# One program text for all engines in a two-layer cross-attention kernel: value steps left whole, 63 pairs of row maxima joined

## The reference, cut to what matters

```python
q = (hidden_states @ Wq).reshape(B, Sq, HEADS, head_dim).transpose(0, 2, 1, 3)
k = (encoder_hidden_states @ Wk).reshape(B, Skv, HEADS, head_dim).transpose(0, 2, 1, 3)
v = (encoder_hidden_states @ Wv).reshape(B, Skv, HEADS, head_dim).transpose(0, 2, 1, 3)
scores = jnp.einsum('bhqd,bhkd->bhqk', q, k) / jnp.sqrt(jnp.asarray(head_dim, q.dtype))
probs = jax.nn.softmax(scores, axis=-1)
out = jnp.einsum('bhqk,bhkd->bhqd', probs, v)
out = out.transpose(0, 2, 1, 3).reshape(B, Sq, H) @ Wo + bo
return out + residual
```

## Time and profile before

| | |
|---|---|
| median of 3 runs | 323.26 us |
| span of the profiled execution | 320.5 us |
| median less span | 2.8 us |
| TensorE busy | 308.1 us (96%) |
| VectorE busy | 259.9 us (81%) |
| ScalarE busy | 228.9 us (71%) |
| GpSimd busy | 77.8 us (24%) |

### The profile page before, as it was taken

How to read it: one execution, slowest core, us unless ns; L and a number is a source line. 1 busy time by engine, 2 the same in 40 slices (tenths; PEclk the granted TensorE clock), 3 DMA queues, 4 the chain that set the end, 5 groups by cost and what they waited for, 6 DMA issues and landing times.

```text
span 320.5 us, 6083 instructions
## 1 busy us (share of the span) xinstructions
PE 308.1 (96%) x2086; PEld 166.4 (52%) x2086; DVE 259.9 (81%) x456; ACT 228.9 (71%) x468; POOL 77.8 (24%) x97
## 2 busy tenths in 40 slices
PE   7999999999999999999999999999999999999995
PEld 6678888876766634333344343334433453443335
DVE  1469899889986899998999899998999988893213
ACT  3556456543445797889878988888898877878982
POOL 6055157360434310010013100130441016101030
PEclk9999999999999999999999999999999999999999
DMA  7960007859946831471723817329065010110102
GB/s 228 322 200 0 2 2 199 246 142 179 225 127 204 183 80 54 95 107 52 125 60 76 126 42 124 75 68 125 27 124 92 37 50 30 57 33 26 38 30 83
DMA packets 20193, 32.79 MB, mean 102 GB/s; under 512 B 5539, under 2 KB 9667, under 8 KB 20163
## 3 DMA queue, kind: packets, MB, share of 16 engines
q1 hardware_dynamic: 19075, 31.27, 42.2%
q10 hardware_dynamic: 1088, 1.14, 1.2%
HBM read 20.63 MB, written 11.61 MB: 101 GB/s over the span
## 4 chain that ended last, share of the span: by engine, by line
PE 72%; ACT 9%; DVE 7%; issue 4%; DMA 4%; SPq 3%; POOL 1%; ACTq 0%; POOLq 0%; DVEq 0%
PE ps L1393 19%; PE ps L1370 13%; PE ps L1381 13%; PE ps L1221 10%; PE ps L1042 8%; ACT probs L701 4%; SPq L347 2%; ACT probs_last L701 2%; DVE mx L906 2%; PE ps L1108 2%; DMA QS<-mT 1%; DMA rec_rows<-recs 1%; PE ps L1168 1%; PE ps L1148 1%; DMA QS<-q_parts 1%
## 5 line engine op out<-in xcount | busy, mean ns | idle before, releaser
L906 DVE TENSOR_REDUCE mx<-ps 128x1 f32<-128x512 f32 x298 | 186.1, 683 | 16.3 <-PE ps L1370 14.6
L701 ACT ACTIVATE probs<-ps 128x512 f32<-128x512 f32 x216 | 113.5, 610 | 22.2 <-PE ps L1381 20.9
L1370 PE MATMUL ps<-KS,QS 48*128 48x512 f32 x256 | 77.9, 450 | 2.2 <-ACT probs L701 1.2
L1381 PE MATMUL ps<-QS,KS 50*128 50x512 f32 x256 | 72.1, 440 | 1.6 <-DMA QS<-mT 0.4
L1393 PE MATMUL ps<-probs,VS 128*32 128x512 f32 (+1 forms) x552 | 60.3, 511 | 0.3 <-ACT probs L701 0.3
L701 ACT ACTIVATE probs_last<-ps 128x512 f32<-128x512 f32 x104 | 54.8, 611 | 6.7 <-PE ps L1381 6.2
L1370 PEld LDWEIGHTS ps<-KS,QS 48*128 48x128 f32 x256 | 35.0, 184 | 36.8 <-DVE mx L906 16.2
L1381 PEld LDWEIGHTS ps<-QS,KS 50*128 50x128 f32 x256 | 33.9, 184 | 33.3 <-ACT probs L701 13.5
L1393 PE MATMUL ps<-probs_last,VS 128*32 128x512 f32 (+1 forms) x256 | 29.0, 524 | 0.0
L507 POOL CAST neg_p<-neg 128x16 fp32r<-128x16 f32 x10 | 2.1, 211 | 110.0 <-DVE neg L916 104.3
L683 ACT CAST parts<-ps 128x512 fp32r<-128x512 f32 (+1 forms) x18 | 10.5, 584 | 19.6 <-PE ps L1221 19.4
(11 more groups left out here) (186 smaller groups left out, 440.5 us busy)
## 6 DMA issues: line engine op xcount, KB each, us to landing
KS<-k_parts SPq DMA_DIRECT2D x48, 128.0 KB, 4.7
k_parts<-parts SPq DMA_DIRECT2D x8, 512.0 KB, 3.5
QS<-q_parts SPq DMA_DIRECT2D x48, 64.0 KB, 5.0
raw_rows<-o_raw SPq DMA_DIRECT2D x9, 256.0 KB, 2.0
q_parts<-parts SPq DMA_DIRECT2D x4, 512.0 KB, 3.9
cs<-in_ctx_dram SPq DMA_DIRECT2D x2, 768.0 KB, 9.3
KS_last<-k_parts SPq DMA_DIRECT2D x12, 128.0 KB, 4.6
xs<-in_x_dram SPq DMA_DIRECT2D x2, 640.0 KB, 6.3
```

Source lines behind the costliest of these rows:

```text
L701: act.activation(probs[t % 3][:, h, :], ps[:, bank_of["s", m], :], ACT.Exp, scale=float(D1) ** -0.5).then_inc(exp_done, 1)
L906: dve.tensor_reduce(mx[:, g % BUF, u:u + 1], ps[:, bank_of["m", n], :], AX.X, ALU.max).then_inc(max_done, 1)
L1370: pe.matmul(ps[:, bank, :], QS[g % BUF][rows, pair, qt * P:(qt + 1) * P], KS[g % BUF][rows, pair, half * 512:half * 512 + 512], start=True ...
L1381: pe.matmul(ps[:, bank, :], KS[g % BUF][rows, h // 2, kt * P:(kt + 1) * P], QS[g % BUF][rows, h // 2, :], start=True, stop=True).then_inc( ...
```

## The change

`EARLY`, `PLAN`, `BANKS`, `X_AT` and the rules of the other engines are gone. One text, `PROGRAM`, holds all units in order, and every engine walks it from front to back. Things that were tied to a step's number are now words in it: `o` (ScalarE or VectorE copies a group's output), `send`, `inv`, `pieces`, `chunk`, `stage`, `loadk`, `loadq`, `ones`, `bias0`. Where an order used to follow from the old list, waits are added (on `proj_mm`, `u_mm`, `x1_mm`, `q0_mm`). All 80 values steps are whole; 21 of them were cut before. `M` is a joined pair: 63 instead of 11. A group's value output may lie in any bank. s units may run ahead of the step by more or less than four. `sums` and `recs` have a place of their own in SBUF, and `sums_in` is two semaphores.

```diff
-    EARLY = [("warm", 0, 8), ("xT", 0, 0), ("xT", 0, 1), ("tok",), ("xT", 0, 2), ("w", 0), ("warm", 1, 8), ("kvp", 0), ("kvp", 1),
...
-    JOIN = [1, 5, 7, 39, 101, 173, 233, 263, 274, 295, 318]
-    PLAN = ["m1mmm203vmm", "201m3v", "1mm2m03vm", "m21m03v", "m21m0max3mmb", "m10mamm23bmm", "01mm2m3v", "3m210mmab", "10mmm32mmv",
...
+    PROGRAM = (
+        "bias0:0 warm:0:8 w:0 tok warm:1:8 xT:0:0 xT:0:1 xT:0:2 kvp:0 kvp:1 kvT:0 q0:0:0 q0:0:1 q0:0:2 n0:0 kvT:1 xT:1:0 xT:1:1",
...
+        "3m102mmvmmM301vmM012 loadq:3 3m3vm loadwo 2011mmv neg:1 send:0 MM032vMM02 o:0 1vmmm320 loadq:4 loadk:4 311mmv0mmm inv:0",
...
+    def parsed():
+
+        units, joined, n, m, v = [], set(), 0, 0, 0
+        for word in " ".join(PROGRAM).split():
+            if set(word) <= set("mMv0123ab"):
+                for c in word:
+                    if c in "mM":
+                        if c == "M":
+                            joined.add(n)
+                            units.append(("m", n))
+                            n += 1
+                        units.append(("m", n))
+                        n += 1
+                    elif c in "0123":
+                        units.append(("s", m, int(c)))
+                        m += 1
+                    else:
+                        units.append(("values", v, {"v": None, "a": 0, "b": 1}[c]))
+                        v += c != "a"
...
-            for u in EARLY:
-                leave(u)
-            for h in range(GH):
-                exp(h)
-            for t in range(STEPS):
...
+            for u in units:
+                leave(u)
...
-            def exp(m):
+            def exp(m, h):
...
                 if t >= 3:
                     act.wait_ge(pv_mm, t - 2)
+                elif m == 0:
+                    act.wait_ge(proj_mm, KV0_DONE)
+                elif m == 2 * GH:
+                    act.wait_ge(q0_mm, 6)
```

More of the change, by code:

```diff
@@ new lines, in two_layer_cross_attention @@
+    POOL_FROM = 8
+    def parsed():
[16 more added lines that the diff above has]
+                        v += c != "a"
+            else:
+                kind, *numbers = word.split(":")
+                units.append((kind, *(int(i) for i in numbers)))
+        return units, joined
@@ L101, in two_layer_cross_attention @@
+    units, JOIN = parsed()
     MAXIMA = list(itertools.accumulate(n not in JOIN for n in range(NM)))
-    NEG_STEP = [max([t for t in range(STEPS) if M_FROM[t] < (g + 1) * UNITS], default=-1) for g in range(NG)]
-    X_STEPS = {u: sorted(t for t in X_AT if X_AT[t] == u) for u in X_AT.values()}
+    head_of = {u[1]: u[2] for u in units if u[0] == "s"}
+    NO_BANK = ("loadk", "loadq", "w", "e0", "i0", "n0", "ones", "vones", "bias0", "o", "send", "inv", "pieces", "chunk", "stage",
+               "loadwo", "half", "finB")
@@ L110, in placed @@
         last_in[bank] = u
-    def heads(t):
-        return [int(c) for c in PLAN[t - 1] if c in "0123"] if t else [0, 1, 2, 3]
     def place_all():
-        early_banks = iter(EARLY_BANKS)
-        for u in EARLY:
[L119 to L135, removed]
-                    v += 1
-        for u, bank in zip((u for u in TAIL if u[0] != "finB" and u != ("finA", 7)), TAIL_BANKS):
-            placed(u, int(bank))
-        bank_of["finA", 7] = bank_of["res", 7]
+        banks = iter("".join(BANKS))
+        for u in units:
+            if u[0] == "values":
+                u = ("pv", u[1] // NKT) if u[1] % NKT == 0 and u[2] != 1 else ("values",)
+            if u[0] in NO_BANK or u[0] == "values":
+                continue
+            if u == ("finA", NT - 1):
+                bank_of[u] = bank_of["res", NT - 1]
+            elif u[0] == "m" and u[1] - 1 in JOIN:
+                placed(u, bank_of["m", u[1] - 1] + 1)
+            elif u[0] == "s":
+                placed(u[:2], int(next(banks)))
+            else:
+                placed(u, int(next(banks)))
     place_all()
@@ L151, in two_layer_cross_attention @@
     CHUNK = [(0, 1), (2, 3), (4,), (5, 6), (7, 8)]
-    O_STEP = [at // GH for at in O_AT] + [LATE_O]
+    KV0_DONE = max(proj_no[u] for u in proj_no if u[0] != "q" and u[1] == 0) + 1
+    KV1_DONE = max(proj_no[u] for u in proj_no if u[0] != "q" and u[1] == 1) + 1
+    Q0_DONE = max(proj_no[u] for u in proj_no if u[0] == "q" and u[1] == 0) + 1
     with ExitStack() as ctx:
@@ L579, in chunk_parts @@
                 pool.wait_ge(o_low, c + 1)
-            pool.wait_ge(vs_ready, 1)
-            stage_v(0)
-            for t in range(STEPS):
-                g, kt = t // NKT, t % NKT
-                for c, groups in enumerate(CHUNK):
-                    if t == O_STEP[groups[-1]] + 5:
-                        chunk_parts(c)
-                if kt == 5 and g + 1 < NG:
-                    stage_v(g + 1)
-                if t == WO1_AT:
-                    weight_low(WO1)
-                if t in [n for n in NEG_STEP if n >= 0]:
-                    neg_parts(NEG_STEP.index(t))
-                if t in X_AT and t == X_STEPS[X_AT[t]][-1]:
-                    u = X_AT[t]
-                    if u[0] in ("k", "q") and split_no[u] >= POOL_FROM:
-                        lower_part(u)
-                    elif u[0] == "fin" and u[1] < TB - 1:
-                        final(u[1])
+            for u in units:
+                if u[0] in ("k", "q") and split_no[u] >= POOL_FROM:
+                    lower_part(u)
+                elif u[0] == "m" and u[1] % UNITS == UNITS - 1:
+                    neg_parts(u[1] // UNITS)
+                elif u[0] == "w" and u[1] not in SPLIT_BY_DVE:
+                    weight_low(u[1])
+                elif u[0] == "n0":
+                    normalise0(u[1])
+                elif u[0] == "x1T":
+                    add_bias1(u[1])
+                elif u[0] == "ones":
+                    ones(u[1])
+                elif u[0] == "vones":
+                    value_ones()
+                elif u[0] == "bias0":
+                    add_bias0(u[1])
+                elif u[0] == "chunk":
+                    chunk_parts(u[1])
+                elif u[0] == "stage":
+                    stage_v(u[1])
+                elif u[0] == "fin" and u[1] < TB - 1:
+                    final(u[1])
         @block.scalar
@@ L741, in leave @@
                 if u[0] == "w":
+                    if u[1] == WO1:
+                        act.wait_ge(proj_mm, len(order))
                     weight_high(u[1])
+                elif u[0] == "s":
+                    exp(u[1], u[2])
+                elif u[0] == "o" and u[1] < NG - 2:
+                    copy_o(u[1])
+                elif u[0] == "half":
+                    copy_half(u[1])
+                elif u == ("finB", NT - 1):
+                    copy_last_sums(u[1])
                 elif u[0] == "ftB":
@@ L1019, in leave @@
                     add_last_chunk(u[1])
-            for u in EARLY:
-                leave(u)
-            for t in range(STEPS):
-                g, kt = t // NKT, t % NKT
-                if t == LATE_O:
-                    copy_late_o()
-                if t - 2 in O_STEP:
-                    invert_sums(O_STEP.index(t - 2))
-                for n in range(M_FROM[t], M_FROM[t + 1]):
-                    maximum(n)
-                if t in X_AT and t == X_STEPS[X_AT[t]][-1]:
-                    leave(X_AT[t])
-            for u in TAIL:
+            for u in units:
                 leave(u)
@@ L1321, in unit @@
                     scores(u[1])
+                elif u[0] == "values":
+                    values(u[1], u[2])
                 elif u[0] == "tok":
@@ L1388, in values @@
                 pe.wait_ge(exp_done, GH * t + GH)
-                if kt == 0:
+                if kt == 0 and half != 1:
                     pe.wait_ge(v_staged, g + 1)
@@ L1398, in _ @@
             pe.wait_ge(id_ready, 1)
-            for u in EARLY:
-                unit(u)
-            v = 0
-            for t in range(STEPS):
-                n, m = M_FROM[t], GH * (t + 1)
-                for c in PLAN[t]:
-                    if c == "m":
-                        max_scores(n)
-                        n += 1
-                    elif c in "0123":
-                        scores(m)
-                        m += 1
-                    elif c == "x":
-                        at = X_STEPS[X_AT[t]]
-                        unit(X_AT[t], *((at.index(t), len(at)) if len(at) > 1 else ()))
-                    else:
-                        values(v, {"v": None, "a": 0, "b": 1}[c])
-                        v += c != "a"
-            for u in TAIL:
+            for u in units:
                 unit(u)
```

147 lines of the change are left out of this document (56 added, 91 removed), and 52 rows, old and new, of tables (BANKS, EARLY, PLAN, PROGRAM).

## The result

The changed kernel takes 362.73 us (median of 4 runs, 357.89 to 364.74) against 323.02 us for the kernel before, run beside it (322.23 to 324.06). The ratio is 1.112, with an interval of 1.106 to 1.119: **slower by 11%**. The forecast was 320.6 us, and the range ended at 326.5. The profiled execution took 357.89 us, with a span of 356.2.

The account below looks back on a forecast made before the run. The prediction took VectorE's stream of maxima, 93% full with holes where TensorE comes late, to bound the main stage. Span 320.5 + 3.2 - 3.1 - 2.8 = 317.8, plus 2.8 to the median: 320.6 us; range 315.5 to 326.5.

Parts of the forecast that it names:

- The start: Before layer 0: query-weight work ahead of the token copies delays the first keys product, +3.2 us (bounds 0 and 5).
- Rival 3: TensorE's clock falls in a 2.6 us hole at the start, costing 1.9 us more: 322.5 us; chance 0.08.
- Joined pairs: Main stage, VectorE: each of 51 more joined maxima saves 0.06 us, 3.1 us off.
- All of it counts: Main stage: the full 3.1 us saved on VectorE by joins comes off the time, VectorE being 93% full.
- Rival 4: Main stage: joined pairs choke the banks and make TensorE late, slower, up to 326.5 us; chance 0.17.
- Whole steps: Main stage: 21 uncut values steps save TensorE 0.34 us each, 7.1 us; 2.8 counted, bounds 0 and 4.0.
- The main stage: First values step to last maxima: loses 5.9 us, 3.1 from joins plus 2.8 from TensorE's relief.
- the sign I gave for rival 4: Main stage: VectorE idle 13 us or more, most of it ahead of joined reductions.
- the 2.8 us: Main stage: TensorE's relief closes a fifth of VectorE's 13.2 us of idle time.
- The rest: Output copies, loads, GpSimd and SyncE queues, added waits and tail: nothing counted.
- The added waits, the loads: Added waits met long before; later groups' loads issued at least four values steps ahead of first m unit: nothing.
- The chance of slower: Whole kernel above 324.9 us: 0.20, from choked banks or a bad start with the clock falling or relief unused.

Follow-up runs that it names:

- section 4: section 3's kernel with neg:3, neg:6 earlier (321.16 us); that with maxima taken singly (322.51), 21 steps in halves (326.02), or the change's start (324.39).
- section 5's last kernel: Against section 4's first kernel: neg:3 takes another bank, inv:8 moved behind finC:7, stores of fin:2 and fin:3 later; 321.93 us, ratio 0.996.
- section 1: Kernel before the change with only GpSimd's first two chunks moved, one values step behind their group's output copy instead of five; 347.87 us against 322.73, ratio 1.078.
- section 3: Changed kernel with bank-less words moved so waits stand behind urgent words (pieces behind the next neg), and the earlier kernel's start order; 327.31 us, ratio 1.014.
- section 4's first kernel: section 3's kernel with neg:3 three units and neg:6 two units earlier, their banks with them; 321.16 us, ratio 0.991.

## Why the prediction was wrong, step by step

- **The start (+3.2 us).** Right. The copies ended at 13.1 (forecast 12.76), the first keys product began at 13.15 (12.85), the queries at 16.09 (15.8), the first values step at 113.57 (113.8). Taken alone it costs 3.2 us of the total by medians, 3.7 at like clock (section 4), so the tenth is luck: the queries are 3.5 us later than before (12.60) and the first values step 3.0. Rival 3 had a hole of 2.6 us here; it was 1.3, since the second warm-up took 3.63 us (1.95 before), and the granted clock was 1.00 from 12 to 17 us.
- **Joined pairs (-3.1 us).** Too large, and its sign is barely clear of the noise: 1.4 us for 63 pairs by medians, 0.8 at like clock. The main stage of VectorE is busy 161.3 us instead of 163.9 with them (section 5's last kernel, and the one with single maxima), so 0.045 us for each of 59 joins, where I had 0.06 (the text ahead of the run with single maxima gives the term as 0.15, which it isn't). "All of it counts" was wrong: VectorE has 2.6 us less to do and the kernel gains about half of that. Rival 4 finds no support: with the maxima taken singly, though in the same neighbouring banks, the kernel is no faster.
- **Whole steps (7.1 us of TensorE, of which 2.8 counted).** Right in sign, too small: putting 21 halves back cost 4.9 us (5.7 at like clock), above my bounds for what counts, 0 and 4.0.
- **The main stage (-5.9 us).** With the clock at 1.00 it took 175.0 us in the last kernel, against 179.5 before: -4.5. The sum of the terms was thus near, for the order of TensorE without the words around it, but not by the way I gave: VectorE idles 13.7 us in it (174.98 less 161.28), not about 10, and is busy 5.1 us less than before (166.34), not 3.1. Of its idle time 7.5 us lie ahead of joined reductions, the sign I gave for rival 4, but with single maxima it idles 14.4 us ahead of them, so the joins aren't the reason. The relief thus didn't close VectorE's holes, as the 2.8 us supposed; that the sum came near is in part luck.
- **The rest (nothing).** This is the step that failed. It said that GpSimd and SyncE "idle most of the time: nothing, but if a `pieces` or `stage` came late, the values step behind it would wait, and the cover is gone". The share of idle time says what an engine has left, not when it answers. I read in both queues what was in them, and not what stands in front of what: `chunk:0` was ahead of group 3's negated maxima in the changed text, and `pieces:0`, `pieces:1`, `loadq:5` ahead of its `mT` rows. I also looked for the danger in words that come late; those that hurt came early, and the values step wasn't the victim, but `neg`. The failed term is 0 instead of about 38 us: 362.7 us less the 324.4 of section 4's kernel that keeps the change's start, its whole steps and its pairs, and differs only in where words stand. Of it `pieces` ahead of `neg` is worth 18.7 when it stands alone, and two short distances behind `neg` 6.2. These prices don't add up, since the longer hole hides the shorter one: moving `chunk` alone gave 9.7 us in the change, where its hole of 9.4 us at group 3 only gave way to one of 8.2 for the `mT` rows, and the same kind of move cost 25.1 in the kernel before. The other 3.8 us of the miss (324.4 against the forecast 320.6) are the main stage's gain of 4.5 instead of 5.9 and, for the rest, most likely the clock: that kernel's one run at 1.000 took 322.4 us.
- **The clock.** I weighed it only at the start, at 1.9 us. In the change its mean is 0.936 over 356.2 us, against 1.00. Its price comes on top of the holes': 17.8 us of them went with 25.1 us in section 1.
- **The added waits, the loads (nothing).** I counted at least four values steps from each later load to its first m unit; `loadk:2` has two. It held TensorE for 3.8 us (`KS<-k_parts`), as it stood in SyncE's queue behind the store of the last k, and the hole was gone in the kernel that had it behind `loadq:1`. A second wait, of 1.0 us for queries at 72.06, is still there in the last kernel (at 68.18).
- **The chance of slower (0.20)** went to a mechanism of TensorE and VectorE alone; no rival had an engine that is idle for three quarters of the time.

## What to carry to other kernels

When instructions move between in-order queues, list for each engine, the idle ones first, every instruction that waits for a DMA, and ask what stands behind it and who needs that soonest. A wait whose result is needed late belongs behind the urgent work even if it would be over in time today, since its slack is set by another engine's order. And count for each round trip (here 3.3 us from `neg` to the first s unit) how much work the leading engine has in hand to cover it: two words that left it short by 1.05 and 0.49 us were worth 6.2.

## What the runs showed of the hardware

Behind its long holes TensorE's clock was at half rate for some us: after 9.4 us without a matmul the granted clock was 0.65 over the next 17.6 us (the result), after 8.0 us 0.74 over the next 14 (section 1). Behind a short hole it can fall too: from 166 to 172 us, behind a hole of 1.05 us that ended at 165.36, it was 0.54 (section 3). Yet holes of 0.70, 1.20 and 2.94 us in the profiled execution of the last kernel were followed by no dip, and in the earlier trace rows the clock still stands at 1.00 over the 2.1 us after the end of the work. The Trainium skill (TensorE: Matmul & The Clock Gate, Part 1) says that idleness sends the array back to half rate, and the traces agree with that for the long holes; the length of a hole alone did not tell here which of the short ones would be followed by half clock.

The clock also fell with no hole ahead of it. In the profiled execution of section 4's first kernel TensorE has none over 0.3 us from 162.1 us on, and then:

```profile
224.00:228.00 4.00, 4.00 (x28) 1.90 (x24) 3.67 (x5) 2.91 (x6) 0.00 (x0) 1.00 0.12 25
228.00:232.00 4.00, 4.00 (x18) 1.42 (x19) 2.85 (x4) 3.20 (x7) 0.94 (x1) 0.72 0.13 49
```

18 matmuls instead of 28 in 4 us, on a TensorE that is busy throughout. With the halves put back the clock is 0.50 from 201.5 to 204.5 us, and no hole over 0.05 us lies in the 37 us ahead of it. So that the hole of 1.05 us brought the dip behind it is not shown, only that no dip came there without it. In section 3's kernel the dip from 231.5 us on lies behind a hole of 0.49, and without that hole the clock fell at nearly the same place.
